# Stacks of q from GpSimd's queue to SyncE's, and loads of x to ScalarE's

## What is computed

```python
q = rotary((x @ Wq + bq) as 16 heads of 32);  k = rotary(x @ Wk + bk);  v = x @ Wv + bv   # one k, one v for all heads
attn = softmax(q @ k.T / sqrt(32))
x = layernorm(x + (attn @ v) @ Wo + bo)
hidden = sigmoid(x @ quantize(w1).T) * (x @ quantize(w2).T)        # 512 -> 1408; quantize gives -1, 0 or 1
x = layernorm(x + hidden @ quantize(w3).T)
```

## Time and profile before

| | |
|---|---|
| Median of 3 runs | 600.63 us (598.98 to 602.34) |
| The profiled execution | 601.29 us |
| Its span, first to last instruction | 599.4 us |
| TensorE busy | 546.4 us (91%) |
| VectorE busy | 476.7 us (80%) |
| ScalarE busy | 420.6 us (70%) |
| GpSimd busy | 299.7 us (50%) |
| Granted TensorE clock, mean | 0.972 |

### The profile page before, as it was taken

One profiled execution on the slowest core, in us unless ns is written; L12 is line 12 of the kernel. 1 busy time (PEld: TensorE's weight loads), 2 busy tenths in 40 slices (PEclk: granted clock), 3 DMA queues, 4 the chain that ended last, 5 costly groups with the idle time before them and its releaser, 6 DMA issues.

```text
span 599.4 us, 9184 instructions
## 1 busy us (share of the span) xinstructions
PE 546.4 (91%) x2984; PEld 274.5 (46%) x2984; DVE 476.7 (80%) x639; ACT 420.6 (70%) x857; POOL 299.7 (50%) x398
## 2 busy tenths in 40 slices
PE   9788889898788999999799999999699999989993
PEld 5454445544444444454444445355244444444441
DVE  3788978978998999889989899889989897445433
ACT  2657757779787988787898888678979896233300
POOL 2209796928897734868357335896553300211011
PEclk9779999999979999999999999999799999999997
DMA  8680418239989997999999988989999989000001
GB/s 311 187 310 10 132 41 293 71 65 181 212 147 210 167 181 145 176 193 203 214 199 192 187 163 154 181 187 184 175 217 177 170 177 190 37 0 37 1 0 70
DMA packets 217119, 92.12 MB, mean 154 GB/s; under 512 B 204400, under 2 KB 205552, under 8 KB 216560
## 3 DMA queue, kind: packets, MB, share of 16 engines
q1 hardware_dynamic: 209952, 77.61, 63.9%
q0 software_dynamic: 6144, 12.60, 10.2%
q10 hardware_dynamic: 976, 1.33, 0.6%
HBM read 20.20 MB, written 4.19 MB: 41 GB/s over the span
## 4 chain that ended last, share of the span: by engine, by line
PE 62%; DVE 13%; issue 8%; ACT 8%; DMA 5%; POOL 2%; SPq 1%; ACTq 0%; POOLq 0%; DVEq 0%
PE a_ps L1310 12%; PE b_ps L1310 7%; PE c_ps L1413 7%; PE s_ps L1323 6%; PE s_ps L1355 5%; PE e_ps L1310 5%; DVE p_all L1053 3%; PE b_ps L1323 3%; PE a_ps L1241 3%; DMA pt_sb<-p_all 3%; PE c_ps L1395 3%; ACT p_all L752 2%; PE a_ps L1323 2%; DVE sh_sb L1046 2%; PE s_ps L1366 2%
## 5 line engine op out<-in xcount | busy, mean ns | idle before, releaser
L752 ACT ACTIVATE p_all<-s_ps,sh_sb 128x512 f32<-128x512 f32 x192 | 129.9, 682 | 58.5 <-DVE sh_sb L1046 55.5
L1053 DVE SCALAR_TENSOR_TENSOR p_all<-p_all 128x1024 f16<-128x1024 f32 x96 | 128.6, 1340 | 4.6 <-ACT p_all L760 4.5
L1046 DVE TENSOR_REDUCE sh_sb<-s_ps 128x2 f32<-128x1024 f32 x96 | 116.6, 1215 | 17.2 <-PE s_ps L1355 17.2
L760 ACT ACTIVATE p_all<-p_all 128x1024 f16<-128x1024 f32 x96 | 101.7, 1059 | 2.0
L1310 PE MATMUL a_ps<-late,q 128*128 128x512 f16 x352 | 83.5, 380 | 4.6 <-ACT th L723 2.9
L1355 PE MATMUL s_ps<-k_st,q_st 128*128 128x512 f32 x192 | 79.5, 496 | 2.8 <-ACT p_all L752 1.6
L432 POOL DMA_DIRECT2D q_st<-hi x96 | 49.4, 517 | 59.3 <-PE s_ps L1355 31.4
L561 POOL TENSOR_SCALAR rstd<-mv 128x1 f32<-128x1 f32 x32 | 9.9, 308 | 132.9 <-DVE mv L1013 132.8
L1310 PEld LDWEIGHTS a_ps<-late,q 128*128 128x128 fp8e4 x352 | 31.9, 98 | 47.1 <-issue 7.5
L739 ACT ACTIVATE p_all<-s_ps,sh_sb 128x512 f32<-128x512 f32 x48 | 32.9, 689 | 27.9 <-DVE sh_sb L1040 27.8
L432 POOL DMA_DIRECT2D q_st<-lo x96 | 47.2, 497 | 7.0 <-DVE lo L956 6.7
(11 more groups left out here) (160 smaller groups left out, 1012.0 us busy)
## 6 DMA issues: line engine op xcount, KB each, us to landing
q_st<-hi POOLq DMA_DIRECT2D x96, 64.0 KB, 3.5
q_st<-lo POOLq DMA_DIRECT2D x96, 64.0 KB, 4.3
late<-in_w SPq DMA_DIRECT2D x2, 2816.0 KB, 14.1
xT_sb<-in_xT SPq DMA_DIRECT2D x8, 512.0 KB, 5.4
late<-in_x SPq DMA_DIRECT2D x4, 1024.0 KB, 6.5
out<-late SPq DMA_DIRECT2D x12, 256.0 KB, 2.9
late<-in_w SPq DMA_DIRECT2D x2, 1408.0 KB, 7.1
q_st<-hi SPq DMA_DIRECT2D x32, 64.0 KB, 2.0
```

Source lines behind the costliest of these rows:

```text
L752: act.activation(p_pair[n][:, t % 2, :], pair_banks(h * PAIRS + t // 2)[:, t % 2, :], ACT.Exp, bias=sh_sb[:, 2 * n + t % 2:2 * n + t % 2 + ...
L760: act.activation(p_half[n][:, 0, :], p_pair[n].rearrange("p t k -> p (t k)"), ACT.Copy, scale=P_SCALE).then_inc(p_hi, 1)
L1046: dve.tensor_reduce(sh_sb[:, 2 * n:2 * n + 2], pair_banks(h * PAIRS + i), AX.X, ALU.min).then_inc(maxed, 2)
L1053: dve.scalar_tensor_tensor(out=p_half[n][:, 1, :], in0=p_pair[n].rearrange("p t k -> p (t k)"), scalar=P_SCALE, in1=p_half[n][:, 0, :], op ...
```

## The change

The stacks of sequences 1 to 3 go from GpSimd's queue to SyncE's. Heads 0 to 2 of sequence 1 come ahead of SyncE's loops; all others are issued by a table `STACKS`: at step k, ahead of the transpose of pair k - 1, the stacks of (sequence offset, head). The semaphores of GpSimd's stacks go. The loads of turned x (from sequence 2 on) and of x (from sequence 1 on) go from SyncE's queue to ScalarE's, after its step 6 and its step 12. The order of all other work is the same.

```diff
+STACKS = {1: [(0, 3)], 5: [(0, 4), (0, 5)], 7: [(0, 6)], 9: [(0, 7)], 13: [(0, 8), (0, 9)], 14: [(0, 10)],
+          16: [(0, 11)], 20: [(0, 12)], 21: [(0, 13)], 22: [(0, 14)], 24: [(0, 15)], 28: [(1, 0), (1, 1)], 30: [(1, 2)]}
@@ q_slot
             n = b * H + h
-            if b == 0:
-                return n % QR, q_in[n % QR], (n // QR + 1) * 16 * 4
-            return n % QR, q_by_pool[n % QR], ((n - H) // QR + 1) * 16 * 4
+            return n % QR, q_in[n % QR], (n // QR + 1) * 16 * 4
@@ block.sync
             for t in range(TT):
                 sp.sem_inc(h_free[t], 16)
+            for h in range(HPG - 1):
+                stack(sp, 1, h)
             for b in range(1, B):
                 for k in range(H * PAIRS):
-                    if k == 7 and b < B - 1:
-                        load_xT(b + 1)
+                    for s, h in STACKS.get(k, []):
+                        if b + s < B:
+                            stack(sp, b + s, h)
                     if k:
                         turn(b, *divmod(k - 1, PAIRS))
                     elif b > 1:
                         turn(b - 1, H - 1, 1)
                     if b > 1 and k in (1, 2, 3, 5):
                         store(b - 2, (1, 2, 3, 5).index(k))
-                    if k == 12:
-                        sp.wait_ge(h_ready, b * TT)
-                        load_x(b)
@@ block.gpsimd (every stack(pool, ...) goes; the first and some of the loop are shown)
             cosines(1, "k")
-            stack(pool, 1, 0)
             add_bias(0, 0)
...
             for b in range(1, B):
-                stack(pool, b, 3)
                 if b > 1:
                     inverse_std(b - 2, 1, 2)
                 rotation(b, "q1")
                 if b > 1:
                     inverse_std(b - 2, 1, 3)
-                stack(pool, b, 4)
-                stack(pool, b, 5)
                 rotation(b, "q2")
-                stack(pool, b, 6)
...
                 if b < B - 1:
                     inverse_std(b - 1, 1, 0)
-                    stack(pool, b + 1, 0)
-                    stack(pool, b + 1, 1)
                     inverse_std(b - 1, 1, 1)
                     rotation(b + 1, "k")
-                    stack(pool, b + 1, 2)
@@ block.scalar
+            def load_xT(s):
+                act.wait_ge(*filled("q3", s - 1))
+                for half in range(2):
+                    cols = slice(half * DT * T // 2, (half + 1) * DT * T // 2)
+                    act.dma_start(xT_sb[:, :, :].rearrange("p k t -> p (k t)")[:, cols],
+                                  xT[s, :, cols]).then_inc(xT_in[half], 16)
+
+            def load_x(s):
+                act.wait_ge(h_ready, s * TT)
+                act.dma_start(xb, x[s, :, :].rearrange("(t p) d -> p t d", p=P)).then_inc(x_in, 16)
@@ heads(b) on ScalarE
                     if k == 6:
                         unit(b, "q3")
+                        if b < B - 1:
+                            load_xT(b + 1)
+                    if k == 12:
+                        load_x(b)
                     if k in (6, 7, 9, 10):
                         h_rows(s, (6, 7, 9, 10).index(k))
```

More of the change, by code:

```diff
@@ L328, in layer @@
         q_in = [sem(f"q_in{n}") for n in range(QR)]
-        q_by_pool = [sem(f"q_by_pool{n}") for n in range(QR)]
         scored = sem("scored")
@@ L596, in _ @@
             add_bias(0, 3)
-            for h in range(1, HPG - 1):
-                stack(pool, 1, h)
             for b in range(1, B):
-                stack(pool, b, 3)
                 if b > 1:
@@ L614, in _ @@
                     round_weight(2, 0, 0)
-                stack(pool, b, 7)
                 inverse_std(b - 1, 0, 2)
@@ L619, in _ @@
                     round_weight(2, 2, 1)
-                stack(pool, b, 8)
-                stack(pool, b, 9)
                 rotation(b, "q3")
                 if b == 1:
-                    stack(pool, b, 10)
-                    stack(pool, b, 11)
                     round_weight(2, 1, 2)
@@ L628, in _ @@
                 add_bias(b, 0)
-                if b > 1:
-                    stack(pool, b, 10)
                 add_bias(b, 1)
-                if b > 1:
-                    stack(pool, b, 11)
                 add_bias(b, 2)
                 add_bias(b, 3)
-                for h in range(12, H):
-                    stack(pool, b, h)
                 if b < B - 1:
```

## The result

The changed kernel is slower: 611.78 us (median of 4 runs, 610.42 to 613.0) against 599.81 for the kernel before in the same comparison (4 runs), ratio 1.0184, 95% interval 1.0155 to 1.0214. Forecast were 598.6 us and a range to 605.5. The profiled execution has a span of 610.4 us, against 599.4.

What follows compares the result with a forecast made beforehand. TensorE, busy 546.4 of 599.4 us, was taken as the bound. Terms -1.1 - 0.9 - 0.3 + 0.3 = -2.0 took the profiled 601.29 to 599.3, less 0.66 for the median: 598.6 us; range 594.5 to 605.5.

Steps and rivals of the forecast that it cites:

- Part 1: Stacks leave GpSimd: its rotation of k ends earlier, so TensorE's 1.21 us wait for k_st goes; taken as -1.1 us.
- rival D: At TensorE's waits: each is replaced by one just as late, 600.6 us; chance 7%.
- Part 2: Stacks join SyncE's queue: waits for transposes of pair 12 and of a sequence's end shrink, -0.9 and -0.3 us.
- it fits with little left: On SyncE's queue: a head's two transposes and one stack cost 7.4 of 7.8 us at the median.
- rival B: SyncE is late: double stacks delay pair 12's transpose, adding 3.2 us in sequence 1, 1.6 in sequence 2; 604.6 us, chance 16%.
- Part 3: Loads of x and turned x on ScalarE's queue: seven issues, 3.4 us in all, partly hidden; taken as +0.3 us.
- rival C: ScalarE's load issues are held behind SyncE's transposes, 5 x 2.5 us less idle time; 604.5 us, chance 11%.
- x interleaves instead of standing in front: At pair 12's transpose in sequence 1: x no longer issues ahead of it; a reason for the -0.9 us taken.
- the prediction's own sign: Prediction counts as wrong if TensorE's idle time changes by more than 5 us, or at places not named.
- Rival A: GpSimd's queue clogs the DMA engines; without its stacks transposes land early everywhere and four waits end, 595.9 us; chance 28%.

Runs made afterwards that it cites:

- the stacks alone: The changed kernel with both loads (x and turned x) back on SyncE's queue, so only the stacks move: 605.77 us, ratio 1.0081 to the kernel before.
- after: The profiled execution of the changed kernel, with all moves made: span 610.4 us, against 599.4 for the kernel before.
- The phases of DMAs alone: Kernel before plus, behind its last store, phases of four transposes with or without a load or stack; four transposes by themselves took 11.7 to 11.8 us.
- the execution at 0.975: Another execution of the unmodified changed kernel, with a mean granted clock of 0.975: 610.42 us, 1.8 less than the profiled one.
- the run with turned x alone: The kernel before with only the loads of turned x moved to ScalarE's queue: 605.12 us, ratio 1.0103 [1.0036, 1.017].

## Why the prediction was wrong

**Part 1** was right in its mechanism and brought no time. The wait for k_st went. But in the runs that take away only that wait, TensorE's wait for a last transpose takes its place (3.6 and 2.8 us, in two places each; 0.53 in one before). That is rival D, for this part. I had counted that wait as one that the change would shorten; it is the next bound, and in both runs the stack that was moved near it lengthened it.

**Part 2** had the load of SyncE's queue about right (forecast 7.4 us for a head; stacks and transposes took 7.1 with the stacks alone and 7.5 in after) and drew the wrong conclusion, "it fits with little left". Busy issuing for 92% of the loops, with issues of 1.3 to 7.9 us, the queue does not recover: mean lateness 2.9 us with the stacks alone. Parts 1 and 2 were priced at -2.3 together; the stacks alone measured +4.9 (0.81%). This is rival B in its mechanism, 604.6; B was to decide at one transpose, that of pair 12 of sequence 1. Just that one had no wait: it landed at 190.81, and those who use it had been put off by the stall at 164. In sequences 2 and 3 ScalarE did wait for pair 12, 3.7 and 1.6 us, but with x beside its transposes. In the trace with the stacks alone the waits lay at others: TensorE's 2.0, 2.5 and 0.7 us for the last transposes, and four of ScalarE's of 0.7 to 1.1 us. Only one of these four, for pair 27 of sequence 1, is for a transpose straight behind a double stack; those for pairs 23 and 26 of sequence 3 come behind steps 20, 21, 22 and 24 with a single stack each, which the forecast did not look at. That splitting the double stacks takes 0.65% away is shown by the times; through which waits is not shown, as this trace is the fastest execution.

**Part 3** is the step that failed most. It priced the loads at their issues, +0.3 us, with the transposes' issue as the only bound, and put what a load does to the landing of the DMAs beside it at nothing. Measured, the loads cost 6 us on top of the stacks (1.0184 against 1.0081) and 12.6 alone. The seven issues took 3.9 us in all (3.4 forecast), none over 2, and rival C was false. But moving a load to another queue changes which DMAs are in flight together. In SyncE's queue a load could only be followed by a transpose, never join one being issued. On ScalarE's it did, in each of the five places, though in four of them only for the last 0.1 to 0.7 us of the issue; there it was the next transpose, issued within 1.6 us, that took 5.1 to 6.3 us, with the stacks behind it. The 15.3 us of turned x in sequence 1, with TensorE's stall of 3.44 us for it, come on top. The sentence in part 2 that "x interleaves instead of standing in front" named the mechanism, and booked it as a gain. By the prediction's own sign it is wrong too: TensorE's idle time changed by 6.7 us, over the 5 allowed, and the stall for turned x is at a place not named.

**What the page said.** The Trainium skill (DMA: Bandwidth & Descriptors, Issuing engines are not separate DMA queues) has all issuers share 16 engines, another one saving only sequencer time. The phases of DMAs alone agree in the total (15.1 to 15.3 us by SyncE, 15.0 to 15.9 by ScalarE). The landing of a single transpose is another matter: with the other engines idle 7.6 us at most beside SyncE's load and 9.1 beside ScalarE's, 10.4 and 13.3 with two stacks as well. That an order in one queue protects what stands behind the load is not in that rule; in this kernel, moving x out of it cost 0 to 2.5%, by the queue and the moment. Rival A, with a chance of 28%, is refuted: it expected no stretch near 100 GB/s once the stacks had left GpSimd. After has three in a row at 118 to 124, and the run with the stacks alone one of 81 (382 to 385). Something of it is true all the same: x on ScalarE's queue was dear among GpSimd's stacks, 1.0164, and cost nothing that can be told a step later.

**The clock** was not in the prediction: of the 11.0 us in the profiled executions, 4.3 are TensorE's busy time, with more of it at the lower level. How much of that the stalls bring about is open, by the execution at 0.975 and the run with turned x alone.

**Open.** Why the packets of transposes are slow for up to 9 us when a load joins them and GpSimd's stacks in the loop: by themselves, and beside busy engines, the same DMAs came to 13 us, not to 17 to 21. The 15.4 us in after, with no stack of GpSimd in flight, occurred beside one of seven loads. With the double stacks split it was 8.8; why is not shown. Not run: x a step later with all stacks on SyncE's queue. No version measured here beats the kernel before by more than can be told: the nearest are x a step later on ScalarE's queue (1.0006), two stacks on SyncE's (1.0014) and the split stacks (1.0016).

## What to carry to other kernels

A queue is also an order: before a DMA goes to an idle queue, list what will be in flight when it is issued there, and price the landing of the others beside it, not only the issue. If it has to go there, put it between the bursts of small DMAs; one step made 1.6% here. A queue that is busy for 92% of the time with issues of varying length has to be priced by its lateness at the last of them, not by its mean.

## What the runs showed of the hardware

- A load of 1 MB, alone 5.3 to 5.6 us, with four transposes adds 3.1 to 4.2 us to their 11.7, from whichever queue: in part they overlap.
- In these phases, other engines idle, the longest issue of a transpose was 5.1 to 5.5 us behind SyncE's load and 7.3 to 9.1 beside two stacks and ScalarE's load, with transposes alone 2.4 to 3.6. Beside a stack of GpSimd it was 4.2 to 5.4, behind one of SyncE's own queue 2.6 to 3.5. Plain DMAs were issued in 0.4 to 1.8 us throughout. So what was late beside a load was the transposes' issue, and with it all that stands behind them in their queue.
- The load of x took 5.9 to 8.4 us on SyncE's queue. On ScalarE's it took 5.8 to 8.2 with no stack on GpSimd's queue, 7.3 to 16.7 with six or seven of GpSimd's DMAs in flight at its issue, and on GpSimd's own queue 9.0 to 20.2: the same bytes, at moments that differ by some us.
